# Multiplying ones into an unread bank around attention, and later split steps for batch 1, in a one-core three-layer kernel

## What is computed

```python
x = L0_attn_x                                   # (8, 1024, 256)
x = x + 0.5 * moe(layernorm(x))                 # 8 experts, capacity 512, top-1
x = x + attention(layernorm(x))                 # 16 heads of 16, rms-normed and rotated q, k
x = x + 0.5 * moe(layernorm(x))

# attention
q, k = rope(rms(x @ wq.T)), rope(rms(x @ wk.T)); v = x @ wv.T
y = softmax(q @ k.T / 4 + 1) @ v ; return y @ wproj.T
# moe: each token goes to its argmax expert, if that has room
h = relu(buf_e @ w1 + b1) ; y = h @ w2 + b2
```

## Time and profile before

| | us |
|---|---|
| median of three runs | 2409.92 |
| the three runs | 2408.1, 2409.92, 2428.8 |
| the profiled execution, whole | 2421.01 |
| its span on the core | 2419.2 |
| TensorE busy | 2165.8 (90%) |
| VectorE, ScalarE, GpSimd busy | 1736.3 (72%), 1729.5 (71%), 975.9 (40%) |
| share of TensorE in the chain that ended last | 72% |
| mean granted TensorE clock | 0.928 of 2.4 GHz |

### The profile page before, as it was taken

The page is one execution under the profiler, slowest core; times in us unless marked ns, Lnnn a source line. Parts: engine busy times, 40 slices in busy tenths (PEclk is TensorE's granted clock), DMA queues, the critical chain, the costliest instruction groups (busy, mean ns, idle before and its releaser), DMA issues.

```text
span 2419.2 us, 36415 instructions
## 1 busy us (share of the span) xinstructions
PE 2165.8 (90%) x12974; PEld 1151.4 (48%) x12974; DVE 1736.3 (72%) x2555; ACT 1729.5 (71%) x3390; POOL 975.9 (40%) x1157
## 2 busy tenths in 40 slices
PE   6649974698999999999999999999999999965997
PEld 6638963343444434434444343444444334224896
DVE  5636755676888888798888779888887988413774
ACT  5846654357888788788878878887887887844663
POOL 3754523153273256239226613832751101113442
PEclk9669986578999999999999999999999999966998
DMA  5725321514345334334433434442353324201431
GB/s 200 261 98 183 130 98 53 87 27 97 64 74 112 59 82 100 72 58 108 98 59 86 97 72 64 96 94 54 76 112 58 66 55 107 56 10 62 153 110 62
DMA packets 144901, 218.29 MB, mean 90 GB/s; under 512 B 32224, under 2 KB 100954, under 8 KB 144464
## 3 DMA queue, kind: packets, MB, share of 16 engines
q1 hardware_dynamic: 135504, 199.01, 34.8%
q0 software_dynamic: 9216, 16.95, 2.0%
HBM read 129.59 MB, written 84.80 MB: 89 GB/s over the span
## 4 chain that ended last, share of the span: by engine, by line
PE 72%; DVE 9%; POOL 7%; ACT 4%; issue 4%; DMA 3%; SPq 1%; POOLq 0%; DVEq 0%; ACTq 0%
PE PS L784 18%; PE PS L768 17%; PE PS L751 10%; PE PS L696 5%; DVE NMX L1309 5%; PE PS L572 4%; PE PS L728 3%; PE PS L665 2%; PE PS L666 2%; PE PS L667 2%; PE PS L649 2%; POOL buf L1434 2%; PE PS L604 2%; PE PS L651 2%; PE PS L650 2%
## 5 line engine op out<-in xcount | busy, mean ns | idle before, releaser
L1309 DVE TENSOR_REDUCE NMX<-PS 128x1 f32<-128x1024 f32 x1024 | 1224.5, 1219 | 298.4 <-PE PS L751 292.6
L1000 ACT ACTIVATE PB<-PS 128x512 f32<-128x512 f32 x2048 | 1103.9, 606 | 244.3 <-PE PS L768 236.4
L768 PE MATMUL PS<-QF,KF 51*128 51x512 f32 x2048 | 808.9, 467 | 21.9 <-DMA QF<-MT 8.5
L751 PE MATMUL PS<-KF,QF 49*128 49x512 f32 x2048 | 734.3, 453 | 40.9 <-DVE NMX L1309 28.1
L768 PEld LDWEIGHTS PS<-QF,KF 51*128 51x128 f32 x2048 | 332.1, 187 | 574.6 <-ACT PB L1000 286.1
L784 PE MATMUL PS<-PB,V 128*17 128x512 f32 x4096 | 550.5, 610 | 0.2
L751 PEld LDWEIGHTS PS<-KF,QF 49*128 49x128 f32 x2048 | 320.5, 191 | 177.5 <-DVE NMX L1309 113.4
L1415 POOL TENSOR_TENSOR RS<-VE,NEGH 128x8 f32<-128x8 f32 x24 | 40.2, 1675 | 379.0 <-DVE VE L1105 378.9
L1236 DVE TENSOR_TENSOR HLR<-HL,HHR 128x512 fp32r<-128x512 f32 x128 | 88.6, 692 | 93.6 <-ACT HHR L930 93.6
L1526 POOL TENSOR_TENSOR R1R<-R,HI 128x512 fp32r<-128x512 f32 x56 | 71.7, 1281 | 178.5 <-ACT R L967 178.5
L665 PE MATMUL PS<-W2H,HLR 128*128 128x256 f32 x512 | 143.1, 279 | 0.0
(11 more groups left out here) (171 smaller groups left out, 3246.2 us busy)
## 6 DMA issues: line engine op xcount, KB each, us to landing
W<-in_w SPq DMA_DIRECT2D x32, 1024.0 KB, 8.0
QF<-qs SPq DMA_DIRECT2D x192, 128.0 KB, 4.7
KF<-qs SPq DMA_DIRECT2D x192, 128.0 KB, 7.6
qs<-HI SPq DMA_DIRECT2D x64, 256.0 KB, 2.1
qs<-R1R SPq DMA_DIRECT2D x64, 256.0 KB, 2.5
buf<-ZT SPq DMA_DIRECT2D x16, 520.0 KB, 10.0
BUF<-buf SPq DMA_DIRECT2D x16, 520.0 KB, 8.8
PX<-x2d SPq DMA_DIRECT2D x8, 1024.0 KB, 5.5
```

Of the source, the lines that this page charges most:

```text
L751: m = e.matmul(PS[:, 2 * i + half, :], QF[k][at:at + ROWS_S, p * SEQ + ti * 128:p * SEQ + ti * 128 + 128], KF[k][at:at + ROWS_S, p * SEQ + ...
L768: e.matmul(PS[:, bank, :], KF[k][at:at + ROWS_ST, p * SEQ + sbk * 128:p * SEQ + sbk * 128 + 128], QF[k][at:at + ROWS_ST, p * SEQ + th * 51 ...
L1000: e.activation(PB[j % 3][:, h * 512:(h + 1) * 512], PS[:, place["e", tile], :], ACT.Exp).then_inc(e_out, 1)
L1309: e.tensor_reduce(NMX[:, u % 2, at:at + 1], PS[:, 2 * i:2 * i + 2, :], AX.XY, ALU.max, negate=True).then_inc(s_max, 1)
```

## The change

A helper `again(times, bank)` multiplies the bf16 matrix of ones with itself (K = 128, 512 columns) `times` times into a bank that nobody reads at that moment. It is called

- in steps 13 to 21 of attention (7, 7, 7, 2, 6, 2, 6, 1, 4 products, into bank 7, ahead of the step's side work),
- in each of steps 512 to 533 (3 products, bank 0, after the last `weight` of the step),
- after the last result is evicted (48), after the last projection (30), and four times 2 between the last batch's transposes and logits,
- in both `experts(ph)`: 22 once the last scatter has landed, 6 between the first transposes and the first product with `W1`.

The other part adds 4 to every step of batch 1's `split` on TensorE, ScalarE, GpSimd and SyncE (`FIRST_SPLIT`), and moves the load of batch 1's first unit from step 53 to 56. Cut to its core:

```diff
+FIRST_SPLIT = 4
+AGAIN = (3, 48, 30, 2, 22, 6)
+AGAIN_AT = {**{n: 7 for n in range(13, 16)}, 16: 2, 17: 6, 18: 2, 19: 6, 20: 1, 21: 4}
+def split_at(b, hf, j):
+    return SPLIT_AT[hf][j] + (FIRST_SPLIT if b == 1 else 0)
...
-                        yield SPLIT_AT[hf][j] + 3
+                        yield split_at(b, hf, j) + 3
                         store_q(b, hf, j)
                 if b:
-                    yield EARLY + 52 if b > 1 else 53
+                    yield EARLY + 52 if b > 1 else 56
                     load_unit(4 * b)
...
                 for bank in range(8):
                     take(bank)
+                for i in range(8):
+                    e.wait_ge(scat[i], 16 * NB * (ph + 1))
+                again(AGAIN[4])
                 gathered(NE * ph)
+                again(AGAIN[5])
...
+            def again(times, bank=0):
+                for i in range(times):
+                    e.matmul(PS[:, bank, :], ONES[:, :], ONES[:, :].unsqueeze(1).to_broadcast([128, 4, 128]),
+                             start=True, stop=True)
+            def between():
+                yield LAG + LATE
+                e.wait_ge(pv_out, 2 * NU)
+                again(AGAIN[1])
+                yield PROJ_AT[7] + 1
+                again(AGAIN[2])
+                for g in range(4):
+                    yield LATER.transposes[g] + 1
+                    again(AGAIN[3])
...
+                if n == NS:
+                    side.begin(n, between())
...
+                if n in AGAIN_AT:
+                    again(AGAIN_AT[n], V_BANK)
+                if n == NS:
+                    e.wait_ge(s_max, 32 * NU)
+                if n >= NS and j - LATE < NS:
+                    again(AGAIN[0])
                 side.run(n)
```

More of the change, by code:

```diff
@@ L701, in split @@
                 for hf in range(2):
-                    yield SPLIT_AT[hf][j]
+                    yield split_at(b, hf, j)
                     n = 8 * b + 4 * hf + j
@@ L1285, in split @@
                     if b == 0:
-                        yield SPLIT_AT[hf][j] + 1
+                        yield split_at(b, hf, j) + 1
                         e.wait_ge(sp_raw, n + 1)
```

## The result

| | before | after |
|---|---|---|
| median, us | 2427.82 (20 runs) | 2404.47 (20 runs) |
| lowest, highest | 2407.09, 2432.74 | 2398.30, 2410.09 |
| profiled execution, its span | 2421.01, 2419.2 | 2410.09, 2408.2 |
| mean granted clock | 0.928 | 0.964 |

The ratio is 0.993, with a 95% interval of 0.991 to 0.995: 17 us less, within 1%. (It goes with the means, 2421.6 and 2405.0, and not with the medians, since the times of the kernel before lie in two groups.) The prediction said 2387.6 (2374 to 2403), so the time lies 1.5 us above the range. The kernel before had been shown with three runs (median 2409.92); seventeen more put it at 2427.82. Its 20 times lie in two groups: eight from 2407 to 2411, one at 2417.5, eleven from 2427 to 2433. Those of the changed kernel lie in one.

What follows compares the result with a forecast made beforehand. It took TensorE to bound the middle, with low-clock edges and a stall to gain from: 4.1 + 12.0 + 5.0 + 0.2 + 1.0 = 22.3 us off the 2409.9 median gave 2387.6 us (2374 to 2403).

Steps and rivals of the forecast that it cites:

- The level: Whole kernel: the starting time the gain was taken off, the median of 2409.9 us, not the profiled 2421.0.
- the 22.3 us: Whole kernel: the summed gain of all terms, 4.1 + 12.0 + 5.0 + 0.2 + 1.0.
- the 12.0 for batch 1's pieces: Attention, steps 35 to 38: moving the pieces later removes TensorE's wait for unit 1's maxima, 12.0 us gained (8 to 13).
- the 5.0 for the last steps: Steps 512 to 533: ones slow warm steps but speed up cold ones, 5.0 us gained (-5 to 8).
- The start: Attention, steps 13 to 24: ones raise the clock; 3.0 us lost, 7.1 gained, together 4.1 gained (0 to 7).
- Rival 1: Attention's start: the clock does not follow the ones, giving 2405 us; chance 0.07.
- Rival 4: All ones: weight loads are not hidden, each product costs its load besides, giving 2411 us; chance 0.03.
- What is late next: After batch 1's moved pieces: checked rotation, ScalarE's buffers, later loads and gather; found time to spare or nothing urgent.
- Rival 2: Batch 1's pieces: the stall moves to ScalarE's copies or unit 4's load, up to 8 us back, 2391 to 2396; chance 0.10.
- rival 5: Last steps: clock stays low despite the ones, 2416 us, or over 2450 if it falls at step 512; chance 0.05.
- The gap and the logits: Around the projection and logits: ones mostly hidden in idle time, projection 1.0 us shorter, logits 0.8 lost; 0.2 gained.
- The experts: First rows of both experts: transposes 2.7 us late, products with W1 2.7 gained; 1.0 us gained in both together (bounds ±4).

Runs made afterwards that it cites:

- b1: The kernel before, unchanged, run again on a third chip: 2439.6 us, ratio 1.000.
- b2: The changed kernel, unchanged, run again on the third chip: 2456.2 us, ratio 1.008 against the kernel before.
- f3: b3 with four score-like products, in the scores' places in steps 513 to 533, instead of the last steps' ones: 2397.5 us, ratio 0.984.
- g1: f3 unchanged, run again on a fourth chip: 2404.7 us, ratio 0.986 against the kernel before.
- g2: The changed kernel with its ones in the last 22 steps replaced by f3's four score-like products: 2406.2 us, ratio 0.988.
- f4: f3 with a single product of ones in each of the four places instead of the score-like product: 2418.4 us, ratio 0.992.
- the first job: First set of follow-up runs, on one chip, taking the change apart in four variants; the kernel before took 2425.9 us there.
- e6: b3 without the ones in steps 512 to 533, on a second chip: 2418.4 us, ratio 0.992.
- b3: The changed kernel with batch 1's pieces closer together, ending at step 47 as before the change; third chip: 2446.0 us, ratio 1.003.
- e5: The kernel before plus three ones in each of steps 512 to 533 and the early wait for the scatters: 2465.2 us, ratio 1.011.
- e8: b3 without the 22 and 6 ones at the experts, on the second chip: 2448.6 us, ratio 1.005.
- e9: b3 without the ones in the last steps and at the experts: 2426.3 us, ratio 0.995.
- f1: e6 unchanged, run again in a later job: 2414.5 us, ratio 0.991.
- f2: f1 keeping only the ones at attention's start: 2426.2 us, ratio 0.995.

## Why the prediction was off

**The level.** The forecast hung on 2409.92, the median of three. The third run shown, 2428.8, and the profile's 2421.0 were taken for scatter; they were the more frequent kind. I took the 22.3 us off the lower one. The difference of the two medians is 23.3 us, close to the 22.3 of the sum, but that is luck: the profiles differ by 11.0, and the rest is how often an execution of the kernel before is in its upper group. That these are early falls of the clock in the last steps is likely (b1's profile, with the fall in step 517 in place of 526, takes 76.9 us for them in place of 63.1), but no profile of this chip shows a fall that early.

**The steps that failed** are two terms of the sum: the 12.0 for batch 1's pieces, of which 12.5 came back as a wait for unit 2's maxima at step 52, and the 5.0 for the last steps, which were 0.8. Together they are 15.1 us too high; the other terms, too low by 3.8 in all, make up for a part of it.

**The start: right.** Forecast 4.1, here 5.0 between the two profiles and 4.2 by the means of all. Rival 1 is out: the clock follows in one step. Rival 4 is out too: 22 ones, warm at the end, take 7.79 us with their loads. The Trainium skill ("TensorE: Matmul & The Clock Gate", Part 3) says that a load overlaps a running product only when its row group differs. Taken by itself this doesn't hold here: a load of 98 ns lies under each ones product at 0.23 us from start to start, all rows in use. The same part also names a background weight buffer as a second case in which a load is pulled ahead, and the rows agree with that.

**The pieces: right where I looked, wrong where I didn't.** Forecast 12.0 for the stall, measured 12.6 between steps 35 and 42, and 13.6 from step 24 to 42. "What is late next" went through the rotation, ScalarE's buffers, `load_unit(4)`, `load_unit(3)` and `gather(0)`. It missed that the load of x for batch 2 waits for the last transposition of a piece, and that unit 2's maxima stand behind it: -12.5. Rival 2 had the idea ("the stall moves") with the wrong waits and at most 8 us. The row was there to be read: in the kernel before SyncE issues PX at 605.72 and the maxima at 610.83; four steps later is past the maxima's need.

**The last steps: wrong in size, and in their cause.** I counted 0.25 us a step for three ones, out of 0.76 us of free time; it is 3.06 - 2.58 = 0.47. I put that down to their place, one behind the other after the second pair of `weight`, where they hold up ScalarE's next exponential; no run moved the three alone. And I counted 7.3 us for six cold steps made warm. On the first chip that came true, in the profile and by all the times; the warm steps before them cost it again, and the gain between the profiles of the result is 0.8, not 5. On the second and third chip the ones don't keep the clock up: it falls in steps 515 to 517 with three of them or without, 17 steps of 5.53 are 50 us more than 17 of 2.58, and the last steps lose 29.1 (b1 to b2). This is rival 5. It did not happen in the result, but on these chips; its price was right there ("if it falls right at step 512 ... it is over 2450"; b2 has 2456). What spoke against it, that ones raise TensorE's load, is true and didn't help.

**The gap and the logits: too low.** 0.2 forecast, 2.1 between the two profiles and 3.2 by the means: the logits' 32 products run at 2.4 GHz and are busy 3.9 us in place of 7.0; I had taken the eight ones there as lost time. The projection took 1.3 us longer where the forecast had it 1.0 shorter: the clock fell in the idle time that the ones left ahead of it.

**The experts: right as far as can be told.** 1.0 forecast, 2.5 between the two profiles (0.2 in the first experts, 2.3 from the load's issue to the end in the second), 1.2 by the means. The transposes were to be 2.7 late and were 2.9 in the first experts; the warm products gave it back.

With the prediction's own terms corrected, the first two profiles add up: -0.9 until step 13 (of which -1.3 lie ahead of the first ones), +5.0, +13.6, -12.5 at step 52, +0.6 and +0.8 up to step 533, +4.4 behind it: 11.0, the difference of the spans.

## What to carry to other kernels

A transfer that waits moves everything queued behind it on its engine: when a step is moved, list every instruction of every queue that waits on it, not only those that it issues. Products that are to keep a clock up did best here where the work that they replace stood, in the rows of the array that the real products leave free: a warm step then took 2.60 us in place of 2.58, and the clock was back after 6.8 to 10.2 us (f3, g1, g2). Price a filler in both clocks, and ask what it costs if the clock falls in spite of it; and do not take the level of a kernel from three runs when one of them stands 1% away.

## What the runs showed of the hardware beyond that

- The clock's fall in steps 512 to 533 differs by chip: on the first chip it was in step 526 or not at all in the profiles (times of the kernel before from 2402 to 2434), on the other three in steps 515 to 517 in every profile but f4's (the kernel before: 2431 to 2443; the fourth chip has only g1's and g2's profiles). Why there is open. Whether the result was measured on the chip of the first job is not on record; its times lie in the same two groups.
- The same three chips have in every profile, behind the `weigh` of step 452, a moment in which TensorE, ScalarE and VectorE each wait 1.4 to 3.2 us; the first chip has it in none. Timeline of e6, ScalarE and VectorE:

```profile
1896.70 1.08 ACT L1043 ACTIVATE PB<-PS 128x512 f32<-128x512 f32 x2 [2.34 <-remote]
1896.78 2.36 DVE L1352 TENSOR_REDUCE NMX<-PS 128x1 f32<-128x1024 f32 x2 [2.52 <-remote]
```

  The clock falls at 1895.8 and is back at 1906.1. b2's wait of 2.65 us at step 515 looks the same, with the fall at 2092.2, and so do waits of TensorE of 2.1 to 2.7 us there in b3, e5, e8, g1 and g2. These six have three ones or four products like the scores in a step; the five profiles of these chips without any product added there (e6, e9, f1, f2, b1) have no such wait at step 515, and neither has f3, though the clock falls in all of them. So the clock falls without this wait too, and the cause of the wait is open. Steps 60 to 512 take 1441.5 to 1446.2 us on these chips, 1435.2 to 1438.3 on the first. The trace names no cause, and I tried none.
- Once at 0.50 the clock stayed there for up to 92 us under a TensorE without a break (b2, e5), and came back after 3.4 to 13.7 us at every fall between steps 60 and 512, and after 6.8 to 10.2 in f3, g1 and g2.
